# Where a causal mask enters the score bank: an identity product on TensorE, or a write by ScalarE

## The chip, the cores and the metric

The kernel runs on one core of a Trainium2 chip. The metric is the device time of one execution in microseconds (us). Five engines work from queues of their own and meet at semaphores: TensorE (PE in the profile; its weight loads are PEld), VectorE (DVE), ScalarE (ACT), GpSimd (POOL) and SyncE, which issues DMAs (SPq). Products land in PSUM, in banks of 128 partitions by 512 f32 columns.

## What is computed

One transformer layer over 8 batches of 512 rows of width 512, with 16 heads of width 32: layer norm, causal attention with a rotary table, projection, layer norm and residual, then a feed-forward part with ternary weights, layer norm and residual. What touches the change is this, cut from the reference:

```python
q = _apply_rope(q, cos, sin)
k = _apply_rope(k, cos, sin)
scores = jnp.einsum('bhtd,bhsd->bhts', q, k)
causal = jnp.tril(jnp.ones((T, T), dtype=bool))
scores = jnp.where(causal[None, None], scores, jnp.float32(-jnp.inf))
attn = jax.nn.softmax(scores, axis=-1) * E ** (-0.5)
o = jnp.einsum('bhts,bhsd->bhtd', attn, v)
```

## The kernel before

**Stages.** Every engine runs the same program of iterations j. In iteration j the batch j has its attention (`here`), the batch j - 1 its feed-forward part (`prev`), and the batch j + 1 its queries, keys and values (`nxt`). Attention runs for j = 0 to 7. Iteration 0 has no `prev` and prepares the ternary weights besides (`setup`); iterations 1 to 6 are alike, and 2 to 6 are one loop; iteration 7 has no `nxt`. Each has a first part of 16 steps u (the first product of the feed-forward part, and the row maxima of the scores), then 16 head steps h, then a tail (projection, two layer norms, transposes). The change touches the head steps alone.

**A head's scores.** They are computed transposed, in ten 128x128 blocks, in three PSUM banks `score[0..2]` of 512, 512 and 256 columns. `score[0]` holds the four diagonal blocks, the only ones with a mask. There is one set of three banks, so the next head's products wait until the banks are read. `mask_b` holds one 128x128 block in bf16 (0 or -1e30).

**A head step h**, engine by engine, in the order of the program:
- PE: a filler where there is one, then `scores(h + 1)` (L545, L551), in steps 8 to 13 a `max_pass` for the next batch (L536, into banks of `gen`), then `weigh(h)` (L573: 20 short products of probabilities and values into `pv`). The filler is 12 products of 512 columns (`queries_keys`, L476) in steps 1 to 4, 7, 8, 11 and 12, and 8 or 16 products (`ffn_down`, L519) in steps 5, 6, 9, 10, 13 and 14. Between `scores(1)` and `scores(2)` both kinds stand. Iteration 0 has only the first kind, iteration 7 only the second.
- ACT: `queries_keys` copies a bank of `gen` (L736), then `exponents(h + 1)`: for each of the three banks an Exp to `probs` in f16 (L792) and one in place (L794), then in steps 6, 9 and 13 `final` (L799), a step of the previous batch's last layer norm. In iteration 0 `magnitudes` (L835) and `sign_turned` (L848) stand among them.
- DVE: `qk_low` (L1167) empties the bank that L736 read; in steps 8 to 13 `maxima` (L1068, L1075); `head_output(h)` (L1185, L1187, L1192); and `probs_low(h + 1)`: three subtractions (L942), each of which frees one of the three score banks and counts `s_drained` up by one.
- POOL: three operations for each u (L1431, L1433, L1436) that run on into the head steps, and L1407, L1410, L1452 of `final`.

`scores(h + 1)` starts when the first of the three subtractions of head h has counted `s_drained`: that is `claim_score`. Its parts for `score[1]` and `score[2]` wait for the second and the third. `scores(0)` waits for a DMA of the row maxima besides (`shift_rows`). Every wait holds up all that stands behind it on its engine.

Of the kernel before, what the change touches and what calls it, by code (L numbers as in the profile page):

```python
# [26 lines left out]
BATCHES, T, E, HEADS = 8, 512, 512, 16  # L27
HD = E // HEADS
F = 4 * E
PARTS = 128  # L30
TB = T // PARTS
# [117 lines left out]
def need(eng, semaphore, count):  # L149

    if not isinstance(count, int) or count > 0:
        eng.wait_ge(semaphore, count)


def build(nc, x, w_attn, b_attn, w_proj, b_proj, w_fc, w_down, rope, out):
    f32, f16, bf16 = mybir.dt.float32, mybir.dt.float16, mybir.dt.bfloat16
    ALU = mybir.AluOpType
    ACT = mybir.ActivationFunctionType
# [6 lines left out]
    with ExitStack() as ctx:  # L165
# [3 lines left out]
        def sem(name):  # L169
            return ctx.enter_context(nc.semaphore(name))  # L170
# [99 lines left out]
        c_full, c_ready = sem("c_full"), sem("c_ready")  # L270

        g_full, g_drained = sem("g_full"), sem("g_drained")
        s_full, s_drained = sem("s_full"), sem("s_drained")
        pv_full, pv_drained = sem("pv_full"), sem("pv_drained")
        down_full, down_drained = sem("down_full"), sem("down_drained")
        hsum_full, hsq_full = sem("hsum_full"), sem("hsq_full")
# [141 lines left out]
        def _(pe):  # L418
# [31 lines left out]
            def iteration(j, prev, here, nxt, setup):  # L450
# [13 lines left out]
                def claim_score(use, i):  # L464
                    need(pe, s_drained, s0 + S[use] + i - 2)
                    return score[i]
# [75 lines left out]
                def scores(h):  # L542

                    def part(bank, at, s, t0, t1, start):
                        return nc.tensor.matmul(bank[:, at:at + t1 - t0], qk[0:98, 1, h, PARTS * s:PARTS * (s + 1)],  # L545
                                                qk[0:98, 0, h, t0:t1], start=start, stop=True, skip_group_check=True)
                    if h == 0:
                        pe.wait_ge(k_rows, 16)
                        pe.wait_ge(shift_rows, 32 * (j + 1))
                    bank = claim_score(("scores", h), 0)  # L550
                    nc.tensor.matmul(bank[:, :].rearrange("p (b t) -> p b t", b=TB), identb[:, :],  # L551
                                     mask_b[:, :].unsqueeze(1).to_broadcast([PARTS, TB, PARTS]),
                                     start=True, stop=False, skip_group_check=True)
                    for s in range(TB):
                        mm = part(bank, PARTS * s, s, PARTS * s, PARTS * (s + 1), False)
                    mm.then_inc(s_full, 1)
                    bank = claim_score(("scores", h), 1)
                    part(bank, 0, 0, PARTS, T, True)
                    part(bank, 384, 2, 3 * PARTS, T, False).then_inc(s_full, 1)
                    bank = claim_score(("scores", h), 2)  # L560
                    part(bank, 0, 1, 2 * PARTS, T, True).then_inc(s_full, 1)
# [169 lines left out]
        def _(act):  # L731
# [6 lines left out]
            def iteration(j, prev, here, nxt, setup):  # L738
# [8 lines left out]
                def blocks(bank, n=PARTS):  # L747

                    return bank[:, :].rearrange("p (c t) -> p c t", t=n)
# [28 lines left out]
                def queries_keys(g, which):  # L778
# [3 lines left out]
                    if which == 0:  # L782
# [2 lines left out]
                    high(qkn[:, g % 2, 1 + which, :], bank[:, :], bias=qk_bias[:, EC * which + g:EC * which + g + 1]  # L785
                         ).then_inc(qk_hi, 1)

                def exponents(h):

                    for i, n in enumerate(SCORE_W):  # L790
                        act.wait_ge(s_full, s0 + S["scores", h] + i + 1)
                        nc.scalar.activation(probs[:, h % 2, HI, 512 * i:512 * i + n], score[i][:, 0:n], ACT.Exp,  # L792
                                             scale=1.0 / S_UP)
                        nc.scalar.activation(score[i][:, 0:n], score[i][:, 0:n], ACT.Exp, scale=1.0 / S_UP  # L794
                                             ).then_inc(exp_full, 1)

                def final(tb):
                    act.wait_ge(ln_ready[LF], TB * (j - 1) + tb + 1)
# [53 lines left out]
                for u in range(FC):  # L852
# [10 lines left out]
                    if nxt and u in X_AT:  # L863
# [6 lines left out]
                        if X_AT[u] + 2 < TB:  # L870
                            normalise(X_AT[u] + 2)
                if here:
                    exponents(0)
                if nxt and not here:
                    for c in range(EC):
# [638 lines left out]
```

## Time and profile before

| what | value |
| --- | --- |
| time of the runs | 1373.27 us median of 3 (1372.75 to 1373.28) |
| the profiled execution, from its first to its last instruction | 1373.9 us |
| the same less the median | 0.6 us |
| PE busy | 1214.5 us (88%) |
| DVE busy | 1011.3 us (74%) |
| ACT busy | 782.5 us (57%) |
| POOL busy | 596.2 us (43%) |
| mean granted TensorE clock | 0.944 of full speed |

The profile is one execution. Times in the rows below count from its first instruction. A row of the timeline gives start, length, engine, line, operation and operands; "x4" is four like instructions put together, and the square bracket is the idle time of the engine before it and what ended it. The rows by line and shape give busy time, mean length of one in ns, then idle time before them. PE instructions overlap, so that a product of 512 columns has a length of 0.38 us though the next one starts 0.22 us after it. Line numbers are those of the kernel before; in the changed kernel L573 is L571, L736 is L734, L792 and L794 are L796 and L798, L799 is L805 and L848 is L854; the new instruction is L789.

### The profile page before, as it was taken

The numbers are of one execution on the slowest core, as the hardware profiler recorded it, in microseconds if no ns is written. First come the engines' busy times: TensorE is split into PE (matmuls) and PEld (weight loads), VectorE is DVE, ScalarE is ACT, GpSimd is POOL, SyncE is SP. The second block draws the span as 40 slices with busy tenths as digits, with TensorE's granted clock in tenths as the row PEclk, the third lists the DMA queues.
The fourth block names the chain that finished last, engine by engine and source line by source line (L and its number), as shares of the span: only waits on it lengthen the run. The fifth ranks groups of instructions, "written<-read, shape, count | busy, mean of one in ns | idle before, by whom it ended". The sixth has DMA issues, their size and how long they took to land.

```text
span 1373.9 us, 27331 instructions
## 1 busy us (share of the span) xinstructions
PE 1214.5 (88%) x9388; PEld 657.4 (48%) x9388; DVE 1011.3 (74%) x2931; ACT 782.5 (57%) x1446; POOL 596.2 (43%) x636
## 2 busy tenths in 40 slices
PE   4755979999999998999989998999989999968796
PEld 2322544455545554555445554555445554544343
DVE  7588886877887787868876787868876787656532
ACT  3334864666466754666456754666466755565480
POOL 5221531691159312871259312961259214951252
PEclk9865889999999999999999999999999999978799
DMA  5451121002210222002300221012300230000000
GB/s 199 124 153 63 41 60 55 1 2 68 80 39 2 55 59 75 1 22 66 100 2 2 55 80 53 1 26 62 100 2 3 55 90 11 2 9 25 30 2 31
DMA packets 49697, 65.54 MB, mean 48 GB/s; under 512 B 8439, under 2 KB 33047, under 8 KB 49052
## 3 DMA queue, kind: packets, MB, share of 16 engines
q1 hardware_dynamic: 49564, 63.78, 15.8%
q8 instruction: 82, 1.34, 0.4%
q14 instruction: 51, 0.42, 0.1%
HBM read 29.90 MB, written 8.39 MB: 28 GB/s over the span
## 4 chain that ended last, share of the span: by engine, by line
PE 58%; DVE 26%; ACT 5%; issue 5%; POOL 3%; DMA 1%; SPq 1%; POOLq 0%; DVEq 0%; ACTq 0%
PE gen L476 25%; PE down L519 15%; DVE score L1075 5%; PE pv L573 5%; PE score L545 5%; DVE hT L942 2%; PE score L551 2%; PE score L536 2%; DVE qkn L1167 2%; POOL rstd L1407 1%; DVE acc_add L1052 1%; PE gen L536 1%; DVE probs L942 1%; ACT qkn L736 1%; DVE mx L1075 1%
## 5 line engine op out<-in xcount | busy, mean ns | idle before, releaser
L1407 POOL TENSOR_TENSOR rstd<-veps,mhalf 128x1 f32<-128x1 f32 (+1 forms) x104 | 68.6, 660 | 504.1 <-DVE veps L1152 389.3
L792 ACT ACTIVATE probs<-score 128x512 f16<-128x512 f32 (+1 forms) x384 | 201.7, 525 | 143.7 <-PE score L545 143.7
L476 PE MATMUL gen<-x2T,t1T 128*128 128x512 f16 x1024 | 247.9, 389 | 4.8 <-DVE hT L942 3.4
L519 PE MATMUL down<-t2T,hT 128*128 128x512 f16 x1024 | 235.1, 382 | 3.6 <-DVE xn L1137 3.6
L942 DVE TENSOR_TENSOR probs<-score,probs 128x512 f16<-128x512 f32 (+1 forms) x384 | 207.0, 591 | 18.3 <-ACT score L794 18.2
L794 ACT ACTIVATE score<-score 128x512 f32<-128x512 f32 (+1 forms) x384 | 204.5, 533 | 0.0
L476 PE MATMUL gen<-xT,wa 128*128 128x512 f16 x768 | 179.4, 385 | 12.3 <-DVE wa L962 8.6
L942 DVE TENSOR_TENSOR hT<-gen,hT 128x512 f16<-128x512 f32 x160 | 108.7, 686 | 74.0 <-ACT gen L755 32.1
L1075 DVE CUSTOM_DVE_ANT_0 score<-score,mask_rows 128x512 f32<-128x512 f32 (+1 forms) x344 | 157.7, 519 | 0.0
L476 PEld LDWEIGHTS gen<-x2T,t1T 128*128 128x128 f16 x1024 | 98.4, 100 | 113.2 <-issue 10.9
L754 ACT ACTIVATE hT<-gen,gam 128x512 f16<-128x512 f32 x128 | 87.9, 687 | 112.0 <-PE gen L476 112.0
L519 PEld LDWEIGHTS down<-t2T,hT 128*128 128x128 f16 x1024 | 97.1, 99 | 112.0 <-DVE xn L1137 4.7
L1436 POOL TENSOR_TENSOR acc<-acc,acc_add 128x512 f32<-128x512 f32 x105 | 133.2, 1268 | 8.2
L1431 POOL TENSOR_TENSOR acc_add<-hT 128x512 f32<-128x512 f16 x105 | 121.2, 1154 | 9.6
L476 PEld LDWEIGHTS gen<-xT,wa 128*128 128x128 f16 x768 | 72.4, 99 | 94.6 <-DVE wa L962 9.1
L1433 POOL TENSOR_TENSOR acc_add<-acc_add 128x512 f32<-128x512 f32 x105 | 109.7, 1044 | 8.2
L573 PE MATMUL pv<-v_sb,probs 128*128 128x65 f16 x2560 | 104.6, 198 | 2.5 <-DVE probs L942 2.5
L545 PE MATMUL score<-qk 98*128 98x128 f16 (+2 forms) x896 | 105.9, 253 | 0.0
L573 PEld LDWEIGHTS pv<-v_sb,probs 128*128 128x128 f16 x2560 | 99.2, 101 | 7.4 <-DVE probs L942 2.8
L476 PE MATMUL gen<-wa,xT 128*128 128x512 f16 x384 | 90.2, 386 | 7.0 <-DVE v_bias L942 5.2
L736 ACT ACTIVATE qkn<-gen,qk_bias 128x512 f16<-128x512 f32 x64 | 44.0, 687 | 87.7 <-PE gen L476 72.3
L545 PEld LDWEIGHTS score<-qk 98*128 98x128 f16 x896 | 69.6, 101 | 45.1 <-DVE probs L942 11.5
(131 smaller groups left out, 1861.3 us busy)
## 6 DMA issues: line engine op xcount, KB each, us to landing
qk<-qkn SPq DMA_DIRECT2D x384, 64.0 KB, 2.0
xo<-x SPq DMA_DIRECT2D x8, 1024.0 KB, 5.3
hT<-x SPq DMA_DIRECT2D x8, 1024.0 KB, 6.5
out<-xn SPq DMA_DIRECT2D x32, 256.0 KB, 2.0
hT<-w_fc SPq DMA_DIRECT2D x4, 1024.0 KB, 6.9
hT<-w_down SPq DMA_DIRECT2D x4, 1024.0 KB, 5.0
hT<-w_attn SPq DMA_DIRECT2D x4, 512.0 KB, 10.4
hT<-w_attn SPq DMA_DIRECT2D x1, 1024.0 KB, 8.9
```

Source lines behind the costliest of these rows:

```text
L476: mm = nc.tensor.matmul(bank[:, :], a, b, start=(start and n == 0), stop=(stop and n == len(pairs) - 1))
L519: mm = nc.tensor.matmul(down[:, :], hT[:, half, u, PARTS * tb:PARTS * (tb + 1)], t2T[:, u, :], start=(u == 0 and half == HI), stop=(u == F ...
L545: return nc.tensor.matmul(bank[:, at:at + t1 - t0], qk[0:98, 1, h, PARTS * s:PARTS * (s + 1)], qk[0:98, 0, h, t0:t1], start=start, stop=Tr ...
L573: mm = nc.tensor.matmul(pv[:, VW * tb:VW * (tb + 1)], probs[:, h % 2, half, at:at + PARTS], v_sb[:, s, h, :], start=(s == 0 and half == HI ...
L754: nc.scalar.activation(hT[:, HI, u, :], bank[:, :], ACT.Gelu, scale=gam[:, 0:1])
L792: nc.scalar.activation(probs[:, h % 2, HI, 512 * i:512 * i + n], score[i][:, 0:n], ACT.Exp, scale=1.0 / S_UP)
L794: nc.scalar.activation(score[i][:, 0:n], score[i][:, 0:n], ACT.Exp, scale=1.0 / S_UP).then_inc(exp_full, 1)
L942: return V.tensor_tensor(out, whole, hi, ALU.subtract)
L1075: op = V.tensor_tensor_reduce(part, part, mask_rows[:, T - n:T], 1.0, -3.0e38, ALU.add, ALU.max, mx[:, TB * u + tb:TB * u + tb + 1])
L1431: P.tensor_tensor(whole[:, :], hT[:, HI, u, :], hT[:, LO, u, :], ALU.add).then_inc(sq_step, 1)
L1433: P.tensor_tensor(whole[:, :], whole[:, :], whole[:, :], ALU.mult).then_inc(sq_step, 1 if u else 2)
L1436: P.tensor_tensor(acc[:, :], acc[:, :], acc_add[:, :], ALU.add).then_inc(sq_step, 1)
```

## The change

The identity product with `mask_b` (L551), the first of a head's scores, goes. `mask_bank` on ACT writes the same four mask blocks into `score[0]` with a Copy, and the four diagonal products add to it. ACT waits for the same count of `s_drained` for which PE waited, and PE waits for a new semaphore `mask_set`. ACT's new instruction stands behind `exponents(h)`, ahead of whatever ACT does next; for head 0 it stands ahead of `exponents(0)`.

```diff
@@ tensor @@
-                    bank = claim_score(("scores", h), 0)
-                    nc.tensor.matmul(bank[:, :].rearrange("p (b t) -> p b t", b=TB), identb[:, :],
-                                     mask_b[:, :].unsqueeze(1).to_broadcast([PARTS, TB, PARTS]),
-                                     start=True, stop=False, skip_group_check=True)
+                    pe.wait_ge(mask_set, HEADS * j + h + 1)
+                    bank = score[0]
@@ scalar @@
+                def mask_bank(h):
+
+                    need(act, s_drained, s0 + S["scores", h] - 2)
+                    nc.scalar.activation(blocks(score[0]), mask_b[:, :].unsqueeze(1).to_broadcast([PARTS, TB, PARTS]),
+                                         ACT.Copy).then_inc(mask_set, 1)
+
                 def exponents(h):
...
                         nc.scalar.activation(score[i][:, 0:n], score[i][:, 0:n], ACT.Exp, scale=1.0 / S_UP
                                              ).then_inc(exp_full, 1)
+                    if h + 1 < HEADS:
+                        mask_bank(h + 1)
...
                 if here:
+                    mask_bank(0)
                     exponents(0)
```

On PE in the loop of usual iterations, around `scores(5)`, it stands before as

```order
L476 MATMUL gen<-xT,wa 128x512 [waits g_drained]
L476 MATMUL gen<-xT,wa 128x512 x11
L152 REGISTER_ALU
L551 MATMUL score<-mask_b,identb 128x512 [waits s_drained]
L545 MATMUL score<-qk 128x128 x4
L152 REGISTER_ALU
L545 MATMUL score<-qk 128x384 [waits s_drained]
L545 MATMUL score<-qk 128x128
```

and with the change as

```order
L476 MATMUL gen<-xT,wa 128x512 [waits g_drained]
L476 MATMUL gen<-xT,wa 128x512 x11
L550 REGISTER_ALU
L545 MATMUL score<-qk 128x128 [waits mask_set]
L545 MATMUL score<-qk 128x128 x3
L152 REGISTER_ALU
L545 MATMUL score<-qk 128x384 [waits s_drained]
L545 MATMUL score<-qk 128x128
```

The 512-column product is gone, and the first diagonal product carries the wait for ACT. On ACT in the same loop, from the end of `exponents(7)` in step 6 over `final` to the copy of step 7, it stands before as

```order
L792 ACTIVATE probs<-score 128x256 [waits s_full]
L794 ACTIVATE score<-score 128x256
L798 ISA
L799 ACTIVATE xn<-xn,shift,rstd 128x512 [waits ln_ready3]
L744 REGISTER_ALU
L152 REGISTER_ALU [waits g_full]
L736 ACTIVATE qkn<-gen,qk_bias 128x512 [waits stacked0]
```

and with the change as

```order
L796 ACTIVATE probs<-score 128x256 [waits s_full]
L798 ACTIVATE score<-score 128x256
L789 ACTIVATE score<-mask_b 128x512 [waits s_drained]
L804 ISA
L805 ACTIVATE xn<-xn,shift,rstd 128x512 [waits ln_ready3]
L742 REGISTER_ALU
L152 REGISTER_ALU [waits g_full]
L734 ACTIVATE qkn<-gen,qk_bias 128x512 [waits stacked0]
```

The mask of head 8 waits for DVE ahead of `final` and of the copy of step 7. At the head of `exponents(0)` ACT has, before,

```order
L735 ACTIVATE xT<-gen 128x4x128 [waits g_full]
L792 ACT_TABLE_LOAD
L792 ACTIVATE probs<-score 128x512 [waits s_full]
L794 ACTIVATE score<-score 128x512
```

and with the change

```order
L733 ACTIVATE xT<-gen 128x4x128 [waits g_full]
L789 ACTIVATE score<-mask_b 128x512 [waits s_drained]
L796 ACT_TABLE_LOAD
L796 ACTIVATE probs<-score 128x512 [waits s_full]
L798 ACTIVATE score<-score 128x512
```

The loads of ScalarE's tables stand where they stood, with none added, and the mask of head 0 comes after the last copy of `xT`.

## Rows read from the trace of the kernel before

**Rows 1.** The page: busy time and share of the span.

```profile
PE 1214.5 (88%) x9388; PEld 657.4 (48%) x9388; DVE 1011.3 (74%) x2931; ACT 782.5 (57%) x1446; POOL 596.2 (43%) x636
```

**Rows 2.** Instructions by line and shape: count, busy us, mean ns, idle before, releasers.

```profile
L551 PE MATMUL score<-mask_b,identb 128*128 128x512 bf16 x128 | 50.9, 398 | 35.3 <-DVE probs L942 27.8 <-issue 4.4 <-DMA qk<-m_half 3.1
...
L794 ACT ACTIVATE score<-score 128x512 f32<-128x512 f32 x256 | 153.4, 599 | 0.0
...
L815 ACT ACTIVATE hT<-hT,shift 128x512 f32<-128x512 f32 x32 | 23.0, 718 | 18.8 <-POOL shift L1410 18.6
```

**Rows 3.** Two stretches: length, PE PEld DVE ACT POOL busy, granted clock, DMA.

```profile
589.00:669.00 80.00, 77.80 (x725) 44.29 (x723) 60.34 (x178) 50.08 (x108) 27.18 (x28) 1.00 0.20 53
133.00:213.00 80.00, 63.45 (x621) 40.41 (x622) 64.05 (x178) 59.02 (x117) 27.98 (x16) 0.83 0.21 59
```

**Rows 4.** Timeline of iteration 3 around scores(5): an open head.

```profile
611.40 0.68 DVE L942 TENSOR_TENSOR probs<-score,probs 128x512 f16<-128x512 f32 x1
...
612.01 0.41 ACT L794 ACTIVATE score<-score 128x256 f32<-128x256 f32 x1
...
612.95 0.38 PE L551 MATMUL score<-mask_b,identb 128*128 128x512 bf16 x1
...
613.15 0.69 ACT L736 ACTIVATE qkn<-gen,qk_bias 128x512 f16<-128x512 f32 x1 [0.73 <-PE gen L476]
613.16 0.72 PE L545 MATMUL score<-qk 98*128 98x128 f16 x7
```

**Rows 5.** Timeline of iteration 3 around scores(3): a tight head, and POOL.

```profile
602.67 1.26 POOL L1436 TENSOR_TENSOR acc<-acc,acc_add 128x512 f32<-128x512 f32 x1
603.03 1.05 DVE L1192 TENSOR_TENSOR xo<-oA,r_sum 128x128 f32<-128x128 f32 x1
...
604.00 0.68 DVE L942 TENSOR_TENSOR probs<-score,probs 128x512 f16<-128x512 f32 x1
...
604.73 0.10 PEld L551 LDWEIGHTS score<-mask_b,identb 128*128 128x128 bf16 x1 [0.32 <-DVE probs L942]
...
605.79 0.77 PE L573 MATMUL pv<-v_sb,probs 128*128 128x65 f16 x20
```

**Rows 6.** Timeline of iteration 3 around scores(10): a head between the two.

```profile
635.11 0.68 DVE L942 TENSOR_TENSOR probs<-score,probs 128x512 f16<-128x512 f32 x1
...
636.15 0.38 PE L551 MATMUL score<-mask_b,identb 128*128 128x512 bf16 x1
```

**Rows 7.** Timeline of iteration 3, steps 6 and 7: final ahead of the copy.

```profile
625.47 0.81 ACT L799 ACTIVATE xn<-xn,shift,rstd 128x512 f32<-128x512 f32 x1 [1.26 <-POOL shift L1410]
...
626.38 0.69 ACT L736 ACTIVATE qkn<-gen,qk_bias 128x512 f16<-128x512 f32 x1
...
627.11 0.75 DVE L1167 SCALAR_TENSOR_TENSOR qkn<-gen,qk_bias,qkn 128x512 f16<-128x512 f32 x1 [0.25 <-ACT qkn L736]
```

**Rows 8.** Timeline of iteration 3 around scores(12): DVE's subtraction, ACT's copy.

```profile
645.68 0.68 DVE L942 TENSOR_TENSOR probs<-score,probs 128x512 f16<-128x512 f32 x1
...
646.73 0.69 ACT L736 ACTIVATE qkn<-gen,qk_bias 128x512 f16<-128x512 f32 x1 [1.89 <-PE gen L476]
```

**Rows 9.** Timeline of iteration 0: scores(0), ACT's queue, magnitudes, the subtraction after it.

```profile
133.94 0.52 PE L545 MATMUL score<-qk 98*128 98x128 f16 x3
...
134.64 0.58 ACT L735 ACTIVATE xT<-gen 128x512 f16<-128x512 f32 x1
...
135.12 0.59 ACT L792 ACTIVATE probs<-score 128x512 f16<-128x512 f32 x1
...
140.61 1.91 ACT L835 ACTIVATE x2T<-hT 128x2048 f16<-128x2048 f32 x1
140.76 0.68 DVE L942 TENSOR_TENSOR probs<-score,probs 128x512 f16<-128x512 f32 x1
```

**Rows 10.** Timeline of a tail: PE waits for an ACT instruction.

```profile
1146.31 0.80 ACT L822 ACTIVATE xn<-x,shift,rstd 128x512 f32<-128x512 f32 x1
...
1147.24 0.32 PE L471 MATMUL gen<-ident,xn 128*128 128x128 f32 x1 [0.78 <-ACT xn L822]
```

## What the change will do: the prediction

> **What bounds the kernel now.** The page first: PE is busy for 88% of the span, DVE for 74%, ACT for 57% [rows 1]. That asks for work to be moved from PE to ACT. The two stretches say where it may help. In the head steps of a usual iteration PE is busy 77.8 of 80 us at the full clock of 2.4 GHz, in those of iteration 0 only 63.5 of 80, at 0.83 of it [rows 3]. Then the operation itself: there are 128 identity products, and PE stood idle for 35.3 us ahead of them, 27.8 of these until DVE had freed the bank [rows 2]. So this place on PE is not only work but also a meeting point with DVE, and ACT is now put between the two.
>
> What decides is the slack of a head: from the end of DVE's first subtraction (the bank is free) to the start of L551 (PE is ready). I read it from the timeline, head by head.
> - scores(5): free at 611.40 + 0.68 = 612.08, L551 at 612.95. Slack 0.87, **open** [rows 4].
> - scores(10): free at 635.79, L551 at 636.15. Slack 0.36, **between** [rows 6].
> - scores(3): free at 604.68, weight load of L551 at 604.73 with PE waiting. Slack 0.06, **tight** [rows 5].
>
> Iteration 3 stands for the six usual ones. Its heads 1, 2, 5, 6 and 9 are open, 3 and 7 tight, 8, 12 and 13 nearly so (0.17), and 4, 10, 11, 14 and 15 between (0.36 to 0.60). Head 0 waits for a DMA. In iteration 7 nine heads are tight and seven open.
>
> **What goes.** L551 holds PE from 612.95 to the next product at 613.16, so 0.21 us at full clock, and 128 x 0.21 = 27 us in all [rows 4]. (Its length of 0.38 us overlaps the next.)
>
> **What comes.** A Copy of 512 columns on ACT. No row shows one from a bf16 tile in SBUF into PSUM. From below it is bounded by the 0.60 us of L794, PSUM to PSUM, and from above by the 0.72 us of L815, SBUF to SBUF with a bias operand that the Copy has not [rows 2]. I take 0.60, since it too has constants for operands. Two hand-overs replace one. DVE to PE takes 0.05 us (604.68 to 604.73) [rows 5]; ACT to DVE 0.04 (626.38 + 0.69 = 627.07 to 627.11) [rows 7]; ACT to PE, where PE has another wait besides, 0.13 (1147.11 to 1147.24) [rows 10]. Both new waits are single, so I take 0.04 and 0.05, with 0.02 from weight load to product. The first diagonal product can start 0.04 + 0.60 + 0.05 + 0.02 = 0.71 us after the bank is free, and not before PE is ready. The bounds of this path are 0.69 and 0.72 + 0.13 + 0.13 = 0.98.
>
> The Trainium skill (ScalarE: Activation LUTs, What ACT_TABLE_LOAD costs) gives an ACTIVATE with constant operands as 186 ns + 0.833 ns a column, 0.61 us here, against the 0.60 of L794. By it the sum would rise by under 1 us.
>
> **What follows per head.** The next step's pace hangs on when `weigh` starts. The seven score products last 0.72 us, of which the last one overhangs by 0.17, so `weigh` starts 0.55 after the first of them [rows 4]. In a tight head the second and third subtraction hold them up, and it starts at 605.79, 1.11 after the bank was free [rows 5].
> - Open: PE goes on at once. 0.21 gained.
> - Tight: 0.71 + 0.55 = 1.26 against 1.11. 0.15 lost.
> - Between: at slack 0.36 the start was 0.36 + 0.21 + 0.55 = 1.12, now 1.26: 0.14 lost; at 0.60 a loss turns into 0.1 gained.
>
> Three things come on top, since ACT has a queue.
> 1. ACT may still be in `exponents` when the bank is free. At scores(5) its last Exp ends at 612.42 [rows 4], the mask at 613.0, and PE gets it at 613.06 instead of 612.95: half of the gain is gone. Heads 4 and 5 give 0.16 together. At tight head 7 the same costs 0.27 in place of 0.15.
> 2. The mask of head 8 goes ahead of `final` and the copy of step 7. L799 ran at 625.47 and the copy at 626.38, 0.45 after the bank was free [rows 7]. Now it is mask to 626.57, `final` to 627.3, copy 0.8 later. DVE had waited for that copy (0.25 idle), and with `exponents(8)` behind it too DVE falls back. I count 0.16 for head 8 and 0.2 for head 9, as PE has 0.9 of slack there.
> 3. The copies of steps 11 and 12 start 0.37 after the bank is free (646.36 to 646.73) [rows 8]. ACT is taken until 0.54, and DVE, PE's `max_pass` and the next filler hang on the copy: 0.16 lost at each, heads 12 and 13.
>
> Sum of a usual iteration, losses positive: heads 0 to 2 -0.64; 3 +0.15; 4 and 5 -0.16; 6 -0.21; 7 +0.27; 8 +0.16; 9 +0.2; 10 and 11 +0.07 together (DVE is the longer path there); 12 and 13 +0.32; 14 and 15 +0.07. That is **+0.2 us**, six times +1.4. Iteration 7: seven open heads -1.5, nine tight ones at 0.15 to 0.27 +1.8, **+0.3**.
>
> Iteration 0 is dearer. ACT is late there: its last `xT` copy starts at 134.64 and `exponents(0)` at 135.12, while PE had its first score product out at 133.94 [rows 9]. Now the mask takes 135.12 to 135.72 and that product starts at 135.8, 1.9 later; `exponents(0)` starts some 1.4 later. The mask of head 1 also waits for all six Exps (four of 0.60 and two of 0.41, each 0.1 into the next: 2.6 us), where PE needed two of them and a subtraction (1.7): 0.9 more, 2.3 so far. Then L835, 1.9 us long, started at 140.61 before the bank was free at 141.44 [rows 9]; now it stands behind the mask of head 2, so it starts 1.4 us later against its surroundings, and copy and Exps of the step stand behind it: some 1.2 more. The remaining heads, with L848 behind a mask in eight of them, give 0.5. **+4.0**, with bounds of 2 and 7.
>
> The other things ACT holds up behind a mask are covered: `final` of steps 9 and 13 feeds POOL and a store that are needed a stage later, and the mask of head 0 in later iterations falls into ACT's wait for the row maxima's DMA.
>
> Total: 1.4 + 0.3 + 4.0 = +5.7. The span of 1373.9 lies 0.6 above the median; I add to the median and get **1379.0**.
>
> **Rivals.**
> - *All of PE's time comes back* (4%): the path is hidden in every head, 1373.3 - 27 = 1346. Against it speak the 27.8 us for which PE already waited here.
> - *DVE slips in ahead of POOL* (26%): in step 2 L1192 lasts 1.05 us and ends just when POOL's L1436 does (604.08, 603.93); I take it that it was held up [rows 5]. Heads 0 to 2 come 0.64 earlier, at 602.4, before L1436 starts at 602.67. Then head 3 opens and a usual iteration ends near -0.25: -1.5 + 0.3 + 3 to 4, so 1375 to 1376, no change. The Trainium skill (SBUF — State Buffer, Who interferes with whom) says that a VectorE instruction with two inputs in SBUF and a GpSimd one that reads SBUF shut each other out, the first to issue winning; the row agrees.
> - *Iteration 0 absorbs its delay*, its copies and weights being bound elsewhere, besides (10%): -1.5 to -6, so 1368 to 1371.
> - *The hand-over is long* (18%): at 0.86 instead of 0.71 each of some nine waiting heads loses 0.15 more, 1.3 in a usual iteration: 1379 + 8 = 1387. It decides from a path of 0.87 on, the slack of the open heads behind a copy.
> - *The table is loaded anew for each Copy*: no loads are added in the program's order, so no chance.
>
> **Chances.** The forecast (1376 to 1383) holds 42%. Slower by over 0.2%, that is above 1376.0, has 42 + 18 = 60%; within 0.2% (what a measurement of this kernel can tell) 26%; faster 4 + 10 = 14%. The range of 1368 to 1389 leaves out the first rival and the ends of the others.
>
> **What would show it.** In the profile after: L789 of 0.60 us, 128 times; first diagonal products 0.71 us after the subtraction in tight heads and at the filler's end in open ones; a copy of step 7 some 0.8 us later against the subtraction; scores(0) of iteration 0 at 135.8; L551's 27.8 us of waiting turned into a larger wait of L545 for ACT. The usual iteration, from one scores(0) to the next, moves by under 0.5. I am wrong if it shortens by over 1 us, or if iteration 0 grows by under 2.

## The result: slower, by more than twice the forecast

I had forecast 1379.0, +5.7. The direction was right and the time lies in the range, but the sum was some 7 us short, 8 by the medians.

The profiled execution of the changed kernel has a span of 1382.0 and a time of 1383.84, so 1.8 us lie around the span. The span of 1373.9 shown ahead of the prediction belongs, by that, to an execution of about 1375.7, 2.4 above that kernel's median. The two traces are therefore only 8.1 us apart. Executions of one kernel on one chip spread over 3 to 11 us in what follows, and a part of the reason is found below.

### The profile page after: what moved, and what is told of

Its sections match the earlier page's. It is cut to its first block, busy times and chain, and to the rows that moved or that the text cites. A ratio compares the mean times of both kernels' runs of the same rounds, so it can differ in the third digit from the quotient of the medians.

```text
span 1382.0 us, 27208 instructions
## 1 busy us (share of the span) xinstructions
PE 1189.7 (86%) x9260; PEld 641.6 (46%) x9260; DVE 1009.3 (73%) x2931; ACT 848.8 (61%) x1574; POOL 593.7 (43%) x636
## 4 chain that ended last, share of the span: by engine, by line
PE 43%; DVE 30%; ACT 14%; issue 7%; POOL 3%; DMA 1%; SPq 1%; DVEq 0%; ACTq 0%; POOLq 0%
PE gen L476 18%; PE down L519 11%; DVE score L1082 5%; PE score L545 4%; DVE gen L1082 3%; PE pv L571 3%; ACT probs L796 3%; ACT score L798 2%; ACT score L789 2%; DVE probs L949 2%; DVE hT L949 2%; PE score L536 2%; ACT qkn L734 2%; DVE mx L1082 2%; POOL rstd L1414 1%
## 5 line engine op out<-in xcount | busy, mean ns | idle before, releaser
L545 PE MATMUL score<-qk 98*128 98x128 f16 (+2 forms) x896 | 98.1, 252 | 68.3 <-ACT score L789 64.0
L789 ACT ACTIVATE score<-mask_b 128x512 f32<-128x512 bf16 x128 | 77.3, 604 | 100.5 <-DVE probs L949 100.5
L545 PEld LDWEIGHTS score<-qk 98*128 98x128 f16 x896 | 61.2, 101 | 124.6 <-ACT score L789 98.7
```

The costliest lines, as they stand in the source:

```text
L789: nc.scalar.activation(blocks(score[0]), mask_b[:, :].unsqueeze(1).to_broadcast([PARTS, TB, PARTS]), ACT.Copy).then_inc(mask_set, 1)
```

## The profile after

The page: busy time and share of the span, then the chain that ended last. To compare with [rows 1].

```profile
PE 1189.7 (86%) x9260; PEld 641.6 (46%) x9260; DVE 1009.3 (73%) x2931; ACT 848.8 (61%) x1574; POOL 593.7 (43%) x636
...
PE 43%; DVE 30%; ACT 14%; issue 7%; POOL 3%; DMA 1%; SPq 1%; DVEq 0%; ACTq 0%; POOLq 0%
```

PE has 24.8 us of work less and the span grew by 8.1. Instructions by line (count, busy us, mean ns, idle before, releasers), answering [rows 2]:

```profile
L796 ACT ACTIVATE probs<-score 128x512 f16<-128x512 f32 (+1 forms) x384 | 201.5, 525 | 52.6 <-PE score L545 52.6
...
L545 PE MATMUL score<-qk 98*128 98x128 f16 (+2 forms) x896 | 98.1, 252 | 68.3 <-ACT score L789 64.0 <-DMA qk<-m_half 2.2 <-issue 1.4
...
L789 ACT ACTIVATE score<-mask_b 128x512 f32<-128x512 bf16 x128 | 77.3, 604 | 100.5 <-DVE probs L949 100.5
```

The mask (L789) is 128 instructions of 0.604 us. PE's wait at this place was 27.8 us for DVE, and is 64.0 for ACT. The two stretches of [rows 3], moved to the same heads (length, PE PEld DVE ACT POOL busy, granted clock, DMA):

```profile
593.00:673.00 80.00, 74.77 (x709) 41.92 (x708) 59.99 (x176) 57.79 (x124) 26.76 (x27) 1.00 0.17 43
135.00:215.00 80.00, 56.77 (x600) 37.44 (x601) 63.14 (x175) 63.43 (x127) 27.96 (x16) 0.86 0.17 46
```

Head 3 of iteration 3, the place of [rows 5] (timeline: start us, us, engine, line, out<-in, count, idle before and its releaser):

```profile
606.45 1.27 POOL L1443 TENSOR_TENSOR acc<-acc,acc_add 128x512 f32<-128x512 f32 x1
606.49 1.38 DVE L1199 TENSOR_TENSOR xo<-oA,r_sum 128x128 f32<-128x128 f32 x1
...
607.79 1.61 DVE L949 TENSOR_TENSOR probs<-score,probs 128x512 f16<-128x512 f32 x3
...
608.50 0.60 ACT L789 ACTIVATE score<-mask_b 128x512 f32<-128x512 bf16 x1 [0.75 <-DVE probs L949]
...
609.15 0.56 PE L545 MATMUL score<-qk 98*128 98x128 f16 x5 [1.00 <-ACT score L789]
```

Here is the path that I had costed: the first subtraction ends at 607.79 + 0.68 = 608.47, the mask starts 0.03 later, lasts 0.60, and the first product starts at 609.15. That is 0.68 in all, against the 0.71 forecast (0.69 by the unrounded times, in each of the 62 heads where ACT and PE both stood waiting). In the same rows is something that I had not costed: DVE's step that writes `xo` lasts 1.38 us, until POOL's addition that started 0.04 before it has ended. It was 1.05 in [rows 5].

Two more signs that I had named can be read. In step 7 of iteration 3 the copy starts 1.27 us after the end of the subtraction, where it had been 0.45: 0.82 later, and 0.8 forecast. And scores(0) of iteration 0 starts at 134.99, where I had said 135.8.

The start of the first score product (L545) of a head can be compared in the two traces. This is how much later it came in the changed kernel, in us:

| | head 0 | 3 | 6 | 9 | 12 | 15 |
|---|---|---|---|---|---|---|
| iteration 0 | 1.06 | 2.30 | 2.72 | 1.81 | 1.96 | 3.52 |
| iteration 1 | 3.73 | 3.09 | 2.45 | 3.18 | 3.41 | 3.52 |
| iteration 4 | 3.84 | 4.37 | 3.72 | 4.35 | 4.59 | 4.71 |
| iteration 7 | 5.48 | 6.07 | 5.22 | 5.87 | 5.52 | 7.14 |

It ends 8.1 later. Six usual iterations cost 5.48 - 3.73 = 1.75 (recorded +1.4). The misses are behind iteration 7's first head, 2.7 against 0.3, and the 6 us by which the medians exceed the traces.

## Experiments

Each time below is set against runs of the kernel before on the same chip (medians of 1373.9 to 1375.0). "Head stretch" means the time from the first score product of head 0 to that of head 15, fifteen steps. "+2.5 us" is (ratio - 1) x that median, with its 95% interval in brackets.

### Where does it cost? ScalarE's mask in one kind of iteration at a time

```diff
-                    pe.wait_ge(mask_set, HEADS * j + h + 1)
-                    bank = score[0]
+                    if h in on_act(j):
+                        pe.wait_ge(mask_set, mask_count(j, h))
+                        bank = score[0]
+                    else:
+                        bank = claim_score(("scores", h), 0)
+                        nc.tensor.matmul(bank[:, :].rearrange("p (b t) -> p b t", b=TB), identb[:, :],
...
-                    if h + 1 < HEADS:
+                    if h + 1 < HEADS and h + 1 in on_act(j):
                         mask_bank(h + 1)
```

`on_act(j)` is a tuple of heads for iteration 0, for 1 to 6, and for 7; here all sixteen in one of the three and none in the others.

> ScalarE writes the mask in iterations 1 to 6 only; iterations 0 and 7 keep the identity product. Theory H (the hand-over costs what the trace shows: +3.6 us in iteration 0, +1.75 over the six usual iterations, +2.6 in iteration 7 and its tail; what the medians show beyond these 8 us is time lost in iterations 0 and 7 while PE's granted clock is at half): 1373.3 + 1.8 = 1375, within 0.2% of before. Rival U (the 6 us by which the medians exceed the two traces lie in the usual iterations): about 1381, slower.

Measured: 1376.83, +2.5 us [0.7, 4.3].

> ScalarE writes the mask in iteration 0 only. Theory H: 1373.3 + 3.6 = 1377, the trace showing scores(0) of iteration 0 about 1 us later and its head 15 about 3.5 later. Theory C, a form of H in which the whole rest sits where the clock falls in iteration 0: up to 1383. Rival U: 1377 as well.

Measured: 1379.93, +6.0 us [4.1, 8.0].

> ScalarE writes the mask in iteration 7 only. By my recorded sum +0.3: 1373.6. By the trace +1.7 to head 15 and +2.6 to the end: 1376. Theory H with the clock: 1376 to 1382, with more of iteration 7's heads at half clock than the 27.3 us of before. Rival U: 1376, half clock unchanged.

Measured: 1377.50, +3.8 us [2.3, 5.4].

The three add up to 12.3, and the whole change measured 12.6 on its own chip, so the price is where these say, and U falls: no 6 us more are hidden in the usual iterations. Iteration 7 costs 3.8 where I had recorded 0.3, iteration 0 6.0 for 4.0. Iteration 7 also shows another granted clock. These windows are its head stretch, in the kernel before, in the changed one and in e3_last:

```profile
1196.34:1267.50 71.16, 56.99 (x522) 34.59 (x520) 41.96 (x105) 42.19 (x93) 28.19 (x29) 0.81 0.02 8
```

```profile
1201.82:1274.64 72.82, 53.38 (x506) 34.22 (x506) 41.27 (x105) 50.65 (x108) 27.61 (x29) 0.77 0.02 8
```

```profile
1195.53:1268.95 73.42, 53.88 (x505) 34.23 (x506) 41.36 (x105) 50.64 (x108) 27.61 (x29) 0.77 0.02 8
```

The granted clock (third number from the end) is 0.81 before and 0.77 in both with ScalarE's mask; in e1_usual and e2_first, where iteration 7 keeps the product, it is 0.81 again. The difference is made at the end. From head 0 to head 12 e3_last needs 0.56 us more (57.03 against 56.47) at the same clock of 0.79, from head 12 to head 15 it needs 1.70 more. These last three steps, before and in e3_last:

```profile
1252.81:1267.50 14.69, 13.11 (x118) 7.57 (x116) 9.30 (x25) 8.71 (x19) 1.69 (x3) 0.88 0.00 1
```

```profile
1252.56:1268.95 16.39, 14.17 (x113) 8.51 (x114) 8.79 (x24) 10.43 (x22) 0.95 (x3) 0.70 0.01 1
```

With the product they take 14.69, 14.69 and 14.71 us in three traces (before, e1_usual, e2_first), with ScalarE's mask 16.31 and 16.39 in two. Here are PE's wait in step 12 and the down products of step 13, before and in e3_last:

```profile
1255.98 0.39 PE L551 MATMUL score<-mask_b,identb 128*128 128x512 bf16 x1 [1.58 <-DVE probs L942]
...
1258.31 4.30 PE L519 MATMUL down<-t2T,hT 128*128 128x512 f16 x16
```

```profile
1257.12 1.25 PE L557 MATMUL score<-qk 98*128 98x128 f16 x7 [2.22 <-ACT score L807]
...
1259.28 5.21 PE L531 MATMUL down<-t2T,hT 128*128 128x512 f16 x16
```

PE waits 2.22 us instead of 1.58, and the 16 down products that follow last 5.21 instead of 4.30. That is a correlation as yet, and the mask is not the only thing that moves this clock: e10_light_usual below keeps the product in iteration 7 and shows 0.78 and 70.53 us there, where e9_pool_light, with the same code in this place, shows 0.83 and 68.98.

### Is iteration 7's price the clock?

The test is to take the idle time of PE away and leave the rest of the program as it is: dummy products that nobody reads, put where PE would wait.

```diff
+FILL_AT = {1: 2, 2: 8, 3: 8, 4: 8, 7: 8, 8: 6, 11: 6, 12: 6}
...
+                    if prev and here and not nxt:
+                        for _ in range(FILL_AT.get(h, 0)):
+                            nc.tensor.matmul(gen[general_bank(j, G["up", FC - 1])][:, :], identb[:, :],
+                                             mask_b[:, :].unsqueeze(1).to_broadcast([PARTS, TB, PARTS]),
+                                             start=True, stop=True, skip_group_check=True)
                     if here:
                         if h + 1 < HEADS:
                             scores(h + 1)
```

> The kernel before, with 52 dummy products of 0.21 us (identity x mask into a general bank that nobody reads) in front of the score products of steps 1 to 4, 7, 8, 11 and 12 of iteration 7, where PE stood idle for 1.6 to 2.4 us a step. Theory C (idle PE loses the clock, and the half clock then costs time in the heads that have filler and in weigh): the half-clock stretches in iteration 7's heads go, 27 to 31 us in the trace of before, and the time falls by 5 to 12 us, ratio 0.991 to 0.996. Rival (the clock there costs nothing, as DVE and ACT set the pace): no change, or 1 to 3 us slower through products that don't fit.

Measured: 1366.09, ratio 0.9944 [0.9927, 0.9961]: 5 to 10 us **faster** than the kernel before, with 52 products more.

> ScalarE's mask in iteration 7 only, with the same dummy products. Against e6_before_filled it gives what the hand-over costs in iteration 7 at a steady clock. Theory C: of the 3.8 us of e3_last only 0.3 to 1.5 remain, since the rest was the clock. Rival (the hand-over alone costs it): 3.8 us over e6_before_filled all the same.

Measured: 1366.92, ratio 0.9940 [0.9916, 0.9963]. The same as e6_before_filled, but the two intervals together leave about 4 us open, so the traces have to say it. The same windows, e6_before_filled and e7_last_filled:

```profile
1193.85:1256.04 62.19, 60.10 (x573) 33.00 (x572) 41.43 (x105) 42.17 (x93) 28.14 (x29) 1.00 0.03 10
```

```profile
1199.20:1261.96 62.76, 54.56 (x558) 31.72 (x558) 41.12 (x105) 50.21 (x108) 27.70 (x29) 1.00 0.03 10
```

At full clock iteration 7's fifteen steps take 62.19 us instead of 71.16, and ScalarE's mask adds 0.57 there instead of 2.26 (73.42 - 71.16). To the last instruction it is 3.3 more as it runs (180.8 against 177.5), and 0.4 less with the dummies (169.3 against 169.8). What the half clock costs is seen in step 5, where 16 down products stand. First the kernel before, then e6_before_filled:

```profile
1217.75 0.61 PE L551 MATMUL score<-mask_b,identb 128*128 128x512 bf16 x1 [2.32 <-DVE probs L942]
1218.15 1.27 PE L545 MATMUL score<-qk 98*128 98x128 f16 x7
1219.21 1.31 PE L573 MATMUL pv<-v_sb,probs 128*128 128x65 f16 x20
1220.33 4.52 PE L519 MATMUL down<-t2T,hT 128*128 128x512 f16 x16
```

```profile
1210.67 1.89 PE L683 MATMUL gen<-mask_b,identb 128*128 128x512 bf16 x8
1212.78 0.39 PE L552 MATMUL score<-mask_b,identb 128*128 128x512 bf16 x1 [0.21 <-DVE probs L948]
1213.00 0.99 PE L546 MATMUL score<-qk 98*128 98x128 f16 x7
1213.82 0.77 PE L574 MATMUL pv<-v_sb,probs 128*128 128x65 f16 x20
1214.42 3.62 PE L520 MATMUL down<-t2T,hT 128*128 128x512 f16 x16
```

Before, PE had waited 2.32 us for DVE ahead of this, and 1.9 and 2.5 us in the two steps before it, and was at 1.2 GHz (0.61 for one product) when the wait ended. It then did the step's real work, 16 down products, part of it at half clock, while DVE and ACT waited for the scores behind it. With eight dummies in the wait, 0.21 of it is left, and from the mask product to the end of the down products it is 5.3 us instead of 7.1. So here the wait costs twice: once while it lasts, where DVE's chain covers it, and again in the next step with PE-bound work. Theory C stands for iteration 7, the rival that this clock is worth nothing falls.

### What does the product cost at all?

The diff takes the identity product out of `scores`, lets the first diagonal product start its bank, and takes the exponents of a hundredth of the scores. (A first form, e4_no_mask, with the exponents as they are, gives no time: without a mask some of its probabilities are not finite.)

> No mask at all, in any iteration: the identity product is gone and nothing takes its place, and the exponents are taken of a hundredth of the scores so that the numbers stay finite; the masking is left out. It prices what the product really cost, with no ScalarE instruction and no hand-over. If all of PE's time came back: 27 us less than before, ratio 0.980. If only open and between heads give 0.21 us back (nine to twelve of sixteen): 15 to 20 us less, 0.987. If DVE sets the pace in most heads anyway: under 7 us less, 0.995 or more.

Measured: 1376.52, ratio 1.0008 [0.9991, 1.0025]. With 27 us of products gone and nothing in their place there is **no gain**. The third expectation came nearest. The profiled execution is the slowest of the ten, 1380.71. Part of its time is iteration 0, in which it was granted 0.87 against 0.91. Another part is in the usual iterations, whose head stretch took 73.19 us against 72.49. They gain 0.21 in each open head, as recorded, and lose it again ahead of heads 3, 11, 12 and 15. Between the head stretches of iterations 1 to 7 lie 474.4 us, 472.1 before; why is open. This is the place ahead of scores(11), first in the kernel before, then here (DVE's `xo` step and POOL's last addition of the output):

```profile
640.21 0.29 DVE L1192 TENSOR_TENSOR xo<-oA,r_sum 128x128 f32<-128x128 f32 x1
640.26 1.38 POOL L1452 TENSOR_TENSOR xn<-xn,x 128x512 f32<-128x512 f32 x1 [1.51 <-ACT xn L799]
```

```profile
641.54 1.26 POOL L1449 TENSOR_TENSOR xn<-xn,x 128x512 f32<-128x512 f32 x1 [1.29 <-ACT xn L796]
641.72 1.23 DVE L1189 TENSOR_TENSOR xo<-oA,r_sum 128x128 f32<-128x128 f32 x1
```

Whichever starts first holds the other up. DVE was 0.05 ahead before, and its step took 0.29. Now it is 0.18 behind and takes 1.23, and so the subtraction that frees the bank comes 0.94 later after that step's start.

### Is it POOL that takes the gain?

```diff
+                    cols = slice(0, 8 if u >= 8 else T)
-                        P.tensor_tensor(acc[:, :], acc[:, :], acc_add[:, :], ALU.add).then_inc(sq_step, 1)
+                        P.tensor_tensor(acc[:, cols], acc[:, cols], acc_add[:, cols], ALU.add).then_inc(sq_step, 1)
```

The same `cols` stand in POOL's two other steps of `squares`, and 0:8 in its addition in `finish`.

> The kernel before with POOL cut short where it shares time with the heads: of the sums of squares, units 8 to 15 are done for 8 of 512 columns, and the last addition of the output for 8 columns, so that both are left out in large part. It is the base for the next two. Theory L (DVE and POOL shut each other out of SBUF, and this costs time in the heads): DVE's step that writes xo is 0.29 us long in every head of a usual iteration, and the time falls by some us. Rival: no change.

Measured: 1361.25, ratio 0.9915 [0.9891, 0.9938]. DVE's `xo` step is 0.29 us in all sixteen heads of iterations 1 to 7. But of the 10.5 us that iterations 1 to 6 lose in the trace only 1.9 lie in the head stretches, 8.6 between them; no run here says what POOL's work holds up there. Iteration 3, ahead of scores(3), the place of [rows 5]:

```profile
600.89 0.29 DVE L1192 TENSOR_TENSOR xo<-oA,r_sum 128x128 f32<-128x128 f32 x1
```

> ScalarE's mask in iterations 1 to 6 only, with the same short POOL work. Theory L: the 0.5 us by which head 3 came later than recorded is gone, and a usual iteration changes by 0.1 to -0.4 against e9_pool_light: from -2.5 to +0.5 us. Rival (the 2.5 us of e1_usual are the hand-over and ScalarE's queue alone): +2.5 us over e9_pool_light.

Measured: 1361.56, ratio 0.9913 [0.9887, 0.9940]: 0.3 us over e9_pool_light, with both intervals about 3 us wide on each side. So the medians leave the rival's +2.5 open. The traces speak for theory L: from iteration 1's first score product to iteration 7's it is 896.7 and 896.9 us, and the head stretches are in the table below.

> No mask at all in iterations 1 to 6 (left out, exponents of a hundredth of the scores in all iterations), and the same short POOL work. Without a mask the trace of e5_no_mask gained 0.2 us in each open head and gave it back at heads 10 and 14, where the step that writes xo took 1.2 us beside POOL's addition. Theory L: with POOL short the gain stays, 6 x 16 x 0.21 x 0.6 = 12 us less than e9_pool_light, at least 6. Rival (DVE's own work fills every head): under 3 us less.

Measured: 1349.13, ratio 0.9816 [0.9790, 0.9841]: 12 us under e9_pool_light by the medians, 9 by the two traces, where the removal in all iterations with POOL's full work gave nothing. Theory L had 12, or at least 6. The head stretch of a usual iteration in the traces:

| | POOL as it is | POOL short |
|---|---|---|
| identity product | 72.49 | 72.22 |
| ScalarE's mask | 73.37 | 72.50 |
| no mask | 73.19 | 70.59 |

These are the same to 0.03 us in iterations 3 to 6. ScalarE's mask costs 0.88 us there with POOL's full work and 0.28 with the short one, so 0.60 of it is the meeting with POOL. The gain of 1.63 without a mask is heads 1 to 7 at 0.21 each; heads 8 to 15 give almost nothing even then, as DVE paces them. Six times 1.63 is 9.8, so of the 20 us of products in these six iterations (96 x 0.21) about half was to be had, and that only with POOL's work left out.

### Mask on ScalarE in open heads alone

`on_act` is (0, 1, 2, 6) for iterations 1 to 6, (0, 1, 6, 10, 11, 14, 15) for 7, and empty for 0.

> ScalarE's mask only in heads 0, 1, 2 and 6 of iterations 1 to 6, and 0, 1, 6, 10, 11, 14 and 15 of iteration 7, all open; the identity product elsewhere, and in all of iteration 0. By my recorded per-head figures: -0.85 in each usual iteration and -1.5 in iteration 7, 6.6 us less than before, ratio 0.995. Theory P (what heads 0 to 2 gain is lost again at head 3, where DVE's last step of head 1 now runs into the whole of POOL's addition): -0.2 in a usual iteration and -1.5 in iteration 7, 2 to 3 us less, 0.998.

Measured: 1371.09, ratio 0.9971 [0.9955, 0.9987], 2 to 6 us less than before. Between the two expectations. The head stretch of a usual iteration is 72.04 us in five of six, 0.45 less than before. In the trace iteration 0 is 2.6 us shorter than before, at a clock of 0.94 against 0.91 and with unchanged code, so how much of the gain is the clock's luck in iteration 0 is open here.

### The whole at a steady clock, and the faster version

e12_tail_filled has the dummies of e6, more of them in iteration 7's tail, and ScalarE's mask in heads 0, 1, 2 and 6 of iterations 1 to 6.

> A version meant to be faster: ScalarE's mask in heads 0, 1, 2 and 6 of the usual iterations, the product elsewhere, the dummy products in iteration 7's steps as in e6_before_filled, and in its tail 6 more ahead of the first turn of o, 8 ahead of the last weigh and 8 ahead of each turn of x2. Theory C: the half-clock stretch of 13.7 us at the end of iteration 7 goes too, 2 to 5 us less than e6_before_filled, and 1 to 2 from the heads: ratio to before 0.989 to 0.992. Rival (PE only waits in that tail, so its clock is worth nothing): as e6_before_filled, 0.994.

Measured: 1361.96, ratio 0.9919 [0.9897, 0.9942]. The clock is 1.00 from iteration 7's first score product to 1320 us, and 0.88 in the 34 us that are left. From head 15 of iteration 7 to the end it is 104.7 us, 106.4 before. The ratio is what theory C had at its upper end (0.992), but the interval holds the rival's 0.994 too.

For iteration 0 the dummies go into the general bank that is claimed next:

```diff
+FILL_FIRST = {0: (6, "qk", (0, 0)), 5: (8, "qk", (2, 0)), 6: (3, "qk", (2, 0)), 9: (8, "next max", 3),
+              10: (6, "next max", 6), 13: (10, "next max", 15), 14: (9, "v", 0)}
...
+                    if setup and h in FILL_FIRST:
+                        times, *use = FILL_FIRST[h]
+                        bank = claim(*use)
```

> The kernel before with dummy products wherever PE stood idle in the heads of iterations 0 and 7 and in iteration 7's tail (64 more in the heads of iteration 0 than e12_tail_filled has, 3 to 10 in each of steps 0, 5, 6, 9, 10, 13 and 14, into the general bank that is claimed next). Base for the next. Theory C: half-clock stretches after 145 us are gone but for the last; 1374 - 9 to 10 for iteration 7 - 2 to 4 for iteration 0, so 1360 to 1363, ratio 0.990 to 0.992. Rival (PE only waits in iteration 0, its clock is worth nothing there): 1364 to 1366, 0.9935.

Measured: 1360.20, ratio 0.9888 [0.9870, 0.9906], at the lower end of what theory C had; the rival's 0.9935 falls. So the half clock in iteration 0 does cost the kernel before some us.

> The changed kernel with the same dummy products. Against e13_before_steady it gives the price of the change at a steady clock. Theory C (what the two traces and the medians have over my recorded 5.7 us is the clock): 4 to 7 us, of it 2.5 in the usual iterations, 0.6 in iteration 7, and 2 to 4 in iteration 0. Rival H (the hand-over and ScalarE's queue cost the whole in iteration 0): 2.5 + 0.6 + 5 = 8 us. Rival U (the dummies change nothing of the price): 12 to 13 us.

Measured: 1367.29, ratio 0.9946 [0.9930, 0.9963]: 7.1 us over e13_before_steady by the medians, 8.0 by the ratios, 6.0 by the two spans.

> The faster version again: ScalarE's mask in heads 0, 1, 2 and 6 of the usual iterations alone, with all the dummy products. By e8_open_heads 1 to 3 us less than e13_before_steady: 1358 to 1361, ratio 0.988 to 0.991. Rival (the heads 0 to 2 give back at head 3 what they gain): as e13_before_steady.

Measured: 1359.57, ratio 0.9892 [0.9876, 0.9909]: 0.6 us under e13_before_steady, with intervals of 2 to 2.5 us on each side. The medians can't tell the 1 to 3 us that I expected from the rival's nothing. The traces can say more. From iteration 1's first score product to iteration 7's, in the kernel before, e8_open_heads, e13_before_steady and e15_open_steady:

```profile
289.16:1196.34 907.18, 863.04 (x6903) 467.93 (x6902) 705.51 (x2119) 545.10 (x1036) 417.54 (x458) 0.99 0.15 42
```

```profile
285.43:1190.53 905.10, 860.22 (x6881) 466.43 (x6879) 704.60 (x2120) 558.38 (x1060) 418.73 (x459) 0.99 0.15 42
```

```profile
283.30:1191.30 908.00, 864.83 (x6903) 468.86 (x6902) 704.09 (x2120) 545.04 (x1036) 418.75 (x459) 0.99 0.15 42
```

```profile
284.51:1188.20 903.69, 857.59 (x6880) 465.63 (x6880) 705.51 (x2119) 557.48 (x1059) 416.69 (x458) 0.99 0.15 42
```

Six traces with the product in these iterations lie between 907.1 and 908.0 (before, e2, e3, e6, e7, e13). The three with ScalarE's mask in four open heads took 905.1, 902.2 (e12) and 903.7, the three with it in all heads 908.9 (the changed kernel), 911.1 (e1) and 910.7 (e14). So in the open heads alone it does seem to gain, 2 to 5 us over six iterations, which is one trace each and not shown by a median at a steady clock. In e15 the head stretches gave 1.3 us of it (72.41 each and not 72.04), and the 3.0 between them are only in part explained, by the 0.21 of each head 0 (1.3). e15's iteration 0, whose code is e13's, came out 1.2 us worse, which hides a part of it.

In the price of the whole change, U falls a second time (12 to 13); between C (4 to 7) and H (8) the medians don't decide, but the traces give the parts: 4.5 in iteration 0, 2.7 in iterations 1 to 6, 0.5 in iteration 7's heads, and 1.7 less behind them. The whole of iteration 0, from its first score product to that of iteration 1, in e13_before_steady and e14_after_steady:

```profile
133.11:283.30 150.19, 141.31 (x1166) 77.54 (x1165) 122.83 (x358) 99.01 (x183) 70.66 (x64) 0.98 0.15 43
```

```profile
134.92:287.78 152.86, 135.68 (x1149) 74.99 (x1150) 122.46 (x358) 105.71 (x196) 71.11 (x65) 0.99 0.13 37
```

2.67 longer, and it starts 1.81 later: 4.5 us at a steady clock. Against e15_open_steady, whose code in iteration 0 is that of e13, it is 3.3, so this figure is good to about 1 us. In the kernel before the same stretch is 155.22 at a clock of 0.91:

```profile
133.94:289.16 155.22, 135.78 (x1116) 78.00 (x1115) 123.64 (x358) 99.29 (x183) 71.47 (x65) 0.91 0.14 41
```

The execution of e7_last_filled, with the very same code there, took 158.48 at 0.88 (its row: 133.35 to 291.83), and e6_before_filled 153.66 at 0.94:

```profile
133.35:291.83 158.48, 140.44 (x1116) 80.11 (x1115) 122.72 (x358) 99.34 (x183) 70.53 (x64) 0.88 0.14 40
```

```profile
132.90:286.56 153.66, 133.95 (x1117) 75.77 (x1116) 123.93 (x358) 98.97 (x183) 71.50 (x65) 0.94 0.14 41
```

So the granted clock in iteration 0 differs from execution to execution of the same code, and 5 us go with it. The page's row of the granted clock in tenths, 40 slices of 34 us, for the kernel before and for e13_before_steady, shows where it was low and no longer is (slices 5, 6 and 36 to 38):

```profile
PEclk9865889999999999999999999999999999978799
```

```profile
PEclk9865999999999999999989999999989999999998
```

More of the change, by code:

```diff
@@ L272, in build @@
         g_full, g_drained = sem("g_full"), sem("g_drained")
-        s_full, s_drained = sem("s_full"), sem("s_drained")
+        s_full, s_drained, mask_set = sem("s_full"), sem("s_drained"), sem("mask_set")
         pv_full, pv_drained = sem("pv_full"), sem("pv_drained")
```

## The prediction, step by step

| step | recorded | measured |
|---|---|---|
| bank free to first product | 0.71 us | 0.68 |
| gain in an open head | 0.21 | 0.21 |
| usual iteration, start of head 0 to head 6 | -0.65 | -0.12; -0.70 with POOL short |
| usual iteration, head 6 to head 15 | +1.09 | +0.99; +0.98 with POOL short |
| six usual iterations | +1.4 | +1.75 in the trace (the others: 2.7 and 4.0), +2.5 [0.7, 4.3] |
| iteration 0 | +4.0 | +4.5 or 3.3 at a steady clock, +6.0 [4.1, 8.0] as it runs |
| iteration 7 | +0.3 | +0.6 in the heads at a steady clock, +3.8 [2.3, 5.4] as it runs |

**What held.** The hand-over, the gain of an open head, and the sum of heads 7 to 15, which came within 0.1; there the step "ACT has a queue" matters. Single heads among them are off by up to 0.3 either way (head 7 lost 0.52 for 0.27, head 8 gained 0.12 for a loss of 0.16). Heads 1 to 6 did not hold, by 0.5.

**What failed.** The step "Iteration 7: seven open heads -1.5, nine tight ones ... +0.3". Its terms were right: at full clock it is +0.6. What was missing is that iteration 7 does not run at full clock, and that ScalarE's hand-over adds to the waits of PE behind which the clock is low. The mean clock went from 0.81 to 0.77 over 71 to 73 us, and most of the loss lies between the score products of heads 12 and 15, where PE waited 2.22 us for 1.58 and the down products behind it lasted 5.21 for 4.30. I had read the clock only for iteration 0 [rows 3], as a description, and used it in no term. By the medians the clock made 3.2 us here (3.8 - 0.6; 1.7 to 4.8 by the interval of the 3.8) of the 6.9 that I was short (12.6 - 5.7). That is the largest part, and the only one for which the half clock was taken away and the traces find the price gone. For iteration 0 the same is argued: 4.5 at a steady clock and 6.0 as it runs would be 1.5 more, but the interval of the 6.0 holds 4.5. Of the rest 1.1 are in the usual iterations, 0.5 in iteration 0 and 0.3 in iteration 7. In the usual iterations the meeting with POOL cost 0.5 to 0.6 in each head stretch, for which I had counted nothing, and the time between the head stretches changed by -2.4 us in this trace, -0.3 in e1's and -1.8 in e14's against e13's, where only the 0.21 of each head 0, 1.3 in all, was in my sum.

Within iteration 0 the sum was right for a partly wrong reason. I had put 3.5 on heads 0 to 2 and 0.5 on the others. At head 3 e14 was 2.26 behind e13, at the start of iteration 1 4.48: heads 3 to 15, with queue and hand-over, cost as much as the first three.

**The rivals.** "DVE slips in ahead of POOL" named the right mechanism and the wrong sign. It came true in iteration 1 alone, whose head stretch took 72.40 us against 72.61, with head 3 0.64 earlier and not 0.52 later against head 0. In iterations 2 to 6 DVE came just behind another POOL addition, 0.02 to 0.04 us after its start, and waited for all of it: 1.38 us at 606.49 for 1.05 in [rows 5]. I had moved DVE's step by 0.64 against a POOL instruction that I held fixed, and had not looked at where the next one starts. The Trainium skill (SBUF — State Buffer, Who interferes with whom) has the rule that the first of the two to issue locks the other out; the 1.38, 1.23 and 0.29 above agree with it. "Iteration 0 absorbs its delay" did not come: its start and length together grew by 3.7 us in the trace, 4.5 at a steady clock. (By its own terms that rival's range was 1367 to 1372, not 1368 to 1371.) "The hand-over is long" gave 1387, the measured time, but by a path of 0.86 that is 0.68: the number is a coincidence. "All of PE's time comes back" was further off than its price of 4% said: e5_no_mask had no hand-over at all and came to 1.0008.

**What stays open.** The price of the usual iterations is known to a few us only: three traces with ScalarE's mask in all their heads are 0.9 to 4.0 us over the six with the product, around the 2.5. Whether the clock adds to the change's price in iteration 0 is not shown: its 1.5 us are a difference between +6.0 [4.1, 8.0] and one pair of traces.

## What to carry to other kernels

Before moving work off TensorE, ask what its waits do to its clock: where a stretch shows less than the full clock, the slack read there doesn't price the edit, and filling PE's waits with products nobody reads was worth 14 us (1.1%) here, where moving 27 us of real products away cost 13. Where two engines exclude each other, a gain of tenths of a us upstream only shifts which of two instructions starts first; look for the next instruction of the other engine within the shift, not only for the one that collides now. And a busy share of 88% is no promise: with the product simply left out nothing was gained, so price a removal by leaving the work out first.

## What the runs showed of the hardware

- With a granted clock of 0.81 iteration 7's fifteen steps took 71.2 us, at 1.00 they took 62.2, though 52 dummy products of 0.21 us had been added to them. I had not expected a stretch in which PE waits for DVE in about every second step to hang on PE's clock by 13%.
- A DVE instruction with two SBUF inputs, 0.29 us alone, takes 1.2 to 1.4 beside a POOL addition of 512 columns that starts 0.04 to 0.18 us ahead of it, and ends some 0.15 after it (606.49 + 1.38 against 606.45 + 1.27). It takes 0.29 when it starts 0.05 before (640.21 and 640.26).
- Taking POOL's sums down to 8 columns in half of its units and in the last addition shortened the kernel by 0.85% [0.62, 1.09], with POOL busy 43% of the span and on the chain for 3%. Most of it lies between the head stretches, 8.6 us of 10.5 in the trace.
- A Copy of 512 columns from a bf16 tile in SBUF into PSUM takes 0.604 us, PSUM to PSUM 0.599 (L794); DVE to ACT took 0.03 us and ACT to PE 0.05.
- The same code in iteration 0 took 153.66 us at a granted clock of 0.94 and 158.48 at 0.88, in two executions.
